# Up scaling, copies and additions of the last batch on ScalarE and GpSimd, with new orders in the last step

## The reference

```python
x = x + tanh(g_xattn) * xattn(layernorm(x), ctx, mask, wq, ...)      # ends in a w8a8 linear: round(o / s) @ qw * (s * sw) + b
h = layernorm(x)
qx, sx = quantize(h)                   # per row: max |h| / 448, values rounded as fp8
g = (qx @ qw_gate.T) * scales;  u = (qx @ qw_up.T) * scales
t = silu(g) * u                        # 1408 columns
qt, st = quantize(t)
x = x + tanh(g_ffn) * (qt @ qw_down.T) * scales
```

## Time and profile before

| | |
|---|---|
| median of three runs | 568.79 us (568.49 to 568.90) |
| the profiled execution's own time | 568.58 us |
| its span in the profile | 566.8 us |
| busy in the span: DVE, ACT, PE, POOL | 487.4, 460.9, 443.5, 226.4 us |
| the last step | from about 466 us to the end |

### The profile page before, as it was taken

The page is one execution under the profiler, slowest core; times in us unless marked ns, Lnnn a source line. Parts: engine busy times, 40 slices in busy tenths (PEclk is TensorE's granted clock), DMA queues, the critical chain, the costliest instruction groups (busy, mean ns, idle before and its releaser), DMA issues.

```text
span 566.8 us, 9844 instructions
## 1 busy us (share of the span) xinstructions
PE 443.5 (78%) x3000; PEld 271.9 (48%) x3030; DVE 487.4 (86%) x1254; ACT 460.9 (81%) x1129; POOL 226.4 (40%) x204
## 2 busy tenths in 40 slices
PE   0397495988898889888988987899889975962945
PEld 0274374555545654565456544564556442531312
DVE  5999789988799889988988798879987987789994
ACT  5679799998989798889898988899889985973451
POOL 4432262004552455245524651546155512442620
PEclk9999897999999999999999999999999999896868
DMA  7942352112213221322133203220421011000111
GB/s 254 386 145 77 105 149 56 39 57 39 56 23 87 74 57 22 87 76 57 26 85 74 57 19 90 76 56 16 94 74 20 19 34 57 19 1 0 26 27 75
DMA packets 62085, 39.52 MB, mean 70 GB/s; under 512 B 47568, under 2 KB 53712, under 8 KB 62032
## 3 DMA queue, kind: packets, MB, share of 16 engines
q1 hardware_dynamic: 58432, 31.67, 20.7%
q0 software_dynamic: 2176, 7.22, 4.2%
q10 hardware_dynamic: 1424, 0.01, 0.1%
HBM read 23.87 MB, written 4.19 MB: 50 GB/s over the span
## 4 chain that ended last, share of the span: by engine, by line
DVE 36%; ACT 15%; POOL 14%; issue 11%; PE 8%; DMA 6%; SPq 1%; DVEq 0%; ACTq 0%; POOLq 0%
POOL up L473 5%; POOL up L463 4%; ACT prob L660 3%; DVE q L1209 3%; POOL x L442 3%; DVE ts L1487 3%; ACT q_last L660 2%; DVE q_last L1310 2%; DVE rows L1426 2%; DVE prob L1310 2%; DVE t_sb L1204 2%; DVE stats L1416 2%; DMA t_sb<-in_L_ffn_w_up_dram,index 2%; ACT rows L576 2%; DVE x2s L1431 2%
## 5 line engine op out<-in xcount | busy, mean ns | idle before, releaser
L463 POOL TENSOR_TENSOR up<-up,wgu_scale 128x512 f32<-128x512 f32 (+1 forms) x42 | 52.1, 1241 | 81.4 <-ACT up L640 81.4
L669 ACT ACTIVATE probT<-bank_h 128x512 f32<-128x512 f32 x128 | 68.5, 588 | 1.1 <-PE bank_h L892 0.9
L660 ACT ACTIVATE prob<-prob,neg_max 128x256 f32<-128x256 f32 x128 | 63.3, 497 | 5.5 <-DVE neg_max L1310 5.5
L660 ACT ACTIVATE q_last<-q_last,neg_max 128x256 f32<-128x256 f32 x128 | 63.4, 500 | 0.5 <-DVE neg_max L1310 0.3
L473 POOL TENSOR_TENSOR up<-gate,up 128x512 f32<-128x512 f32 (+1 forms) x42 | 59.5, 1423 | 3.7 <-DVE gate L1365 1.5
L478 POOL TENSOR_TENSOR x<-x,y 128x512 f32<-128x512 f32 x14 | 19.9, 1424 | 101.8 <-DVE y L1500 101.8
L1310 DVE CUSTOM_DVE_ANT_0 prob<-bank_h,mask_sb 128x256 f32<-128x256 f32 x128 | 47.4, 420 | 13.0 <-PE bank_h L833 13.0
L892 PE MATMUL bank_h<-ident,prob 128*128 128x128 f32 x256 | 39.4, 288 | 14.9 <-ACT prob L660 14.8
L1310 DVE CUSTOM_DVE_ANT_0 q_last<-bank_h,mask_sb 128x256 f32<-128x256 f32 x128 | 47.4, 417 | 0.0
L919 PE MATMUL bank_o<-probT,v_sb 128*32 128x256 f32 x512 | 36.0, 400 | 14.4 <-DVE v_sb L1238 8.0
L833 PE MATMUL bank_h<-kf,qf 32*128 32x256 f32 x512 | 36.7, 400 | 11.7 <-ACT probT L669 11.3
(11 more groups left out here) (235 smaller groups left out, 1199.0 us busy)
## 6 DMA issues: line engine op xcount, KB each, us to landing
x_in<-in_x_dram SPq DMA_DIRECT2D x8, 512.0 KB, 3.6
c_in<-in_ctx_dram SPq DMA_DIRECT2D x8, 512.0 KB, 3.8
out_dram<-x SPq DMA_DIRECT2D x7, 512.0 KB, 3.0
mask_sb<-in_mask_BxSxS_ff_dram SPq DMA_DIRECT2D x8, 256.0 KB, 3.1
t_sb<-in_L_ffn_w_down_dram SPq DMA_DIRECT2D x2, 704.0 KB, 5.8
t_sb<-in_L_ffn_w_down_dram POOLq DMA_DIRECT2D x2, 704.0 KB, 6.8
kf<-in_L_xattn_wq_dram SPq DMA_DIRECT2D x1, 1024.0 KB, 10.9
wkT<-in_L_xattn_wk_dram SPq DMA_DIRECT2D x1, 1024.0 KB, 13.7
```

What stands on the lines that cost most here:

```text
L463: pool.tensor_tensor(up[:, c % 2, 0:w], up[:, c % 2, 0:w], wu_scale[:, off:off + w], ALU.mult).then_inc(f["u_scaled"], 1)
L660: ins = act.activation(prob_of[slot4][:, t, :], prob_of[slot4][:, t, :], ACT.Exp, bias=neg_max[:, slot4, t:t + 1], scale=-1.0, accum_out=r ...
L669: act.activation(probT[:, (slot + 3) % 4, :, :].rearrange("p a b -> p (a b)"), HEAD_BANK[(slot + 3) % 4][:, :], ACT.Copy).then_inc(s["turn ...
```

## The change

- `e`'s up scaling leaves `gate_scale` on DVE; `e` now has `up_copy` on ACT and `up_scale` on POOL, as `k`.
- `oqT_low`, `x2T_copy` and the first `tT_low` of `e` move from DVE to ACT; the second `tT_low` stays on DVE.
- The two additions of `x2_add` and the first of the two final additions (`out_add(13)`) of `e` move from DVE to POOL. The second final addition stays on DVE.
- The last batch is stored in two transfers, one per tile, each when its addition is done.
- The orders of all five engines in the last step are written anew. Semaphores are renamed after what they count (low, high).

The diff, cut: for ACT and PE only the new orders are shown, the old ones stand in the kernel above.

```diff
@@ -364,12 +364,13 @@
...
             def tail_order(k):
-                k.o_turn(0); k.o_turn(1); k.out_store(0); k.x2_turn(0); k.x2_turn(1); k.t_turn(2); k.t_turn(0); k.t_turn(1); k.t_turn(3)
-                k.t_turn(4); k.t_turn(5)
+                k.o_turn(0); k.out_store(0); k.o_turn(1); k.x2_turn(0); k.x2_turn(1); k.t_turn(0); k.t_turn(1)
+                k.t_turn(2); k.t_turn(5); k.t_turn(3); k.t_turn(4)
@@ -379,9 +380,11 @@
...
             sp.dma_start(out[bass.ds(NB - 2, 1)].rearrange("o (t p) c -> p (o t) c", p=P), x2[:, :, :]).then_inc(s["stored"], 16)
-            sp.wait_ge(s_last["out_ready"], 1 + 2)
-            sp.dma_start(out[bass.ds(NB - 1, 1)].rearrange("o (t p) c -> p (o t) c", p=P), x_in[:, :, :]).then_inc(s["stored"], 16)
-            sp.wait_ge(s["stored"], 16 * NB)
+            for t in range(NT):
+                sp.wait_ge(s_last["out_ready"], 1 + t + 1)
+                sp.dma_start(out[bass.ds(NB - 1, 1)].rearrange("o (t p) c -> p (o t) c", p=P)[:, t:t + 1, :],
+                             x_in[:, t:t + 1, :]).then_inc(s["stored"], 16)
+            sp.wait_ge(s["stored"], 16 * (NB + 1))
@@ -437,6 +440,8 @@
...
                 def x2_add(slot):
                     need(pool, s["stored"], 16 * B2)
+                    if not OLD:
+                        pool.wait_ge(s["x_centred"], NB)
                     for t in range(NT):
                         pool.wait_ge(f["y_scaled"], 2 * B2 + t + 1)
@@ -465,10 +470,7 @@
                 def gate_up(slot):
                     c = slot - 6
                     w = CHUNKS[c % NCH][1]
-                    if OLD:
-                        pool.wait_ge(f["u_scaled"], 6 * B2 + c + 1)
-                    else:
-                        pool.wait_ge(f["u_ready"], 1 + 6 * B2 + c + 1)
+                    pool.wait_ge(f["u_scaled"], 6 * B2 + c + 1)
                     pool.wait_ge(f["g_ready"], 1 + 6 * B2 + c + 1)
                     pool.tensor_tensor(up[:, c % 2, 0:w], gate[:, c % 2, 0:w], up[:, c % 2, 0:w], ALU.mult).then_inc(f["gu_ready"], 1)
@@ -493,9 +495,10 @@
             def tail_order(k, e):
                 k.x2_add(1); k.x2_var(2); k.up_scale(6); k.gate_up(6); k.up_scale(7); k.gate_up(7); k.up_scale(8)
-                k.gate_up(8); k.up_scale(9); k.gate_up(9); k.up_scale(10); k.gate_up(10); k.up_scale(11); k.gate_up(11)
-                e.x2_var(2); e.gate_up(6); e.gate_up(7); e.gate_up(8); e.gate_up(9); e.gate_up(10); e.gate_up(11)
-                k.out_add(13); k.out_add(15)
+                k.gate_up(8); k.up_scale(9); k.gate_up(9); k.up_scale(10); k.up_scale(11); e.x2_add(1); k.gate_up(10)
+                k.gate_up(11); e.x2_var(2); e.up_scale(6); e.gate_up(6); e.up_scale(7); e.gate_up(7); e.up_scale(8)
+                e.gate_up(8); e.up_scale(9); e.gate_up(9); e.up_scale(10); e.gate_up(10); e.up_scale(11); e.gate_up(11)
+                k.out_add(13); k.out_add(15); e.out_add(13)
@@ -608,7 +611,24 @@
...
-                    act.activation(turned[:, 2 * N:4 * N], U_BANK[:, :], ACT.Identity, bias=-ROUND).then_inc(f["oq_out_act"], 1)
+                    act.activation(turned[:, 2 * N:4 * N], U_BANK[:, :], ACT.Identity, bias=-ROUND).then_inc(f["oq_out_high"], 1)
+
+                def oqT_low(slot):
+                    act.wait_ge(f["oqT_ps"], d - 1)
+                    act.wait_ge(s["q_ps"], 2 * NB)
+                    act.wait_ge(f["d_ps"], 1 + 2 * B2)
+                    act.activation(turned[:, 0:2 * N], G_BANK[:, :], ACT.Identity, bias=-ROUND).then_inc(f["oq_out_low"], 1)
+
+                def x2T_copy(slot):
+                    act.wait_ge(f["x2T_ps"], d - 1)
+                    act.wait_ge(s["v_ps"], 2 * NB)
+                    act.wait_ge(f["u_ps"], 1 + 6 * B2)
+                    act.activation(x2T[:, :, :].rearrange("p c n -> p (c n)"), half(U_BANK), ACT.Copy).then_inc(f["x2T_ready"], 1)
+
+                def tT_low(slot):
+                    act.wait_ge(f["tT_ps"], 1 + 2 * B2 + 1)
+                    act.wait_ge(s["q_ps"], 2 * NB)
+                    act.activation(turned[:, 0:8 * P], half(G_BANK), ACT.Copy).then_inc(f["tT_out_low"], 1)
 
@@ -764,17 +784,19 @@
 
             def tail_order(k, e):
...
+                k.o_int(0); k.head_probT(0); k.head_exp(0); k.head_exp(1); k.head_exp(2); k.head_exp(3); k.head_probT(1)
+                k.head_probT(2); k.head_probT(3); k.head_probT(4); k.head_exp(4); k.group_oT(1); k.x2_mag_0(3)
+                k.head_exp(5); k.group_oT(5); k.head_exp(6); k.head_exp(7); k.head_probT(5); k.head_probT(6)
+                k.head_probT(7); k.head_probT(8); k.up_copy(6); k.x2_mag_1(3); k.gate_tanh(6); k.head_exp(8)
+                k.up_copy(7); k.head_exp(9); k.head_exp(10); k.up_copy(8); k.gate_tanh(7); k.head_exp(11)
+                k.head_probT(9); k.head_probT(10); k.head_probT(11); k.gate_tanh(8); k.group_oT(9); k.up_copy(9)
+                k.head_probT(12); k.gate_tanh(9); k.group_oT(13); k.t_mag_0(10); k.t_mag_1(10); k.up_copy(10)
+                k.o_round(15); e.oqT_high(0); e.oqT_low(0); k.up_copy(11); k.t_mag_2(11); k.gate_tanh(10); e.x2_mag_0(3)
+                e.x2_mag_1(3); k.gate_tanh(11); e.x2T_copy(5); k.t_mag_0(12); e.up_copy(6); k.t_mag_1(12)
+                e.gate_tanh(6); e.up_copy(7); e.up_copy(8); e.gate_tanh(7); k.t_mag_2(13); e.gate_tanh(8); e.up_copy(9)
+                e.up_copy(10); e.gate_tanh(9); e.t_mag_0(10); e.t_mag_1(10); e.up_copy(11); e.gate_tanh(10)
+                e.gate_tanh(11); e.t_mag_2(11); e.t_mag_0(12); e.t_mag_1(12); e.tT_low(12); e.t_mag_2(13); e.tT_high(12)
+                e.tT_high(14)
@@ -1112,17 +1134,17 @@
             def tail_order(k, e):
...
+                k.head_turn(0); k.head_score(0); k.group_pv(1); k.y_project(0); k.head_turn(1); k.head_turn(2)
+                k.head_turn(3); k.head_turn(4); k.head_score(4); k.group_pv(5); k.head_turn(5); k.head_turn(6)
+                k.head_turn(7); k.head_turn(8); k.up_project(5); k.gate_project(5); k.head_score(8); k.up_project(6)
+                k.gate_project(6); k.group_pv(9); k.head_turn(9); k.up_project(7); k.head_turn(10); k.head_turn(11)
+                k.up_project(8); k.gate_project(7); k.gate_project(8); k.head_turn(12); k.group_pv(13); k.o_turn(14)
+                k.gate_project(9); k.up_project(9); k.up_project(10); k.gate_project(10); e.oqT_turn(0); e.y_project(0)
+                e.x2T_turn(5); e.up_project(5); e.gate_project(5); e.up_project(6); e.gate_project(6); e.up_project(7)
+                e.gate_project(7); e.up_project(8); e.gate_project(8); k.down_project_low(12); e.gate_project(9)
+                e.up_project(9); e.gate_project(10); e.up_project(10); k.down_project_high(12); k.down_project_low(14)
+                k.down_project_high(14); e.tT_turn(11); e.down_project_low(12); e.down_project_high(12); e.tT_turn(13)
...
-                def oqT_low(slot):
...
-                    dve.tensor_scalar(turned[:, 0:2 * N], G_BANK[:, :], ROUND, None, ALU.subtract).then_inc(f["oq_out_dve"], 1)
...
-                def x2T_copy(slot):
...
-                    dve.tensor_copy(x2T[:, :, :].rearrange("p c n -> p (c n)"), half(U_BANK)).then_inc(f["x2T_ready"], 1)
...
                 def tT_low(slot):
-                    t = (slot - 12) // 2
-                    dve.wait_ge(f["tT_ps"], 1 + 2 * B2 + t + 1)
-                    if t == 0:
-                        dve.wait_ge(s["q_ps"], at_most(2 * (b + 1), 2 * NB))
-                    else:
-                        dve.wait_ge(f["d_ps"], 1 + 2 * B2 + 1)
-                    dve.tensor_copy(turned[:, 0:8 * P], half(G_BANK)).then_inc(f["tT_out_dve"], 1)
+                    dve.wait_ge(f["tT_ps"], 1 + 2 * B2 + 2)
+                    dve.wait_ge(f["d_ps"], 1 + 2 * B2 + 1)
+                    dve.tensor_copy(turned[:, 0:8 * P], half(G_BANK)).then_inc(f["tT_out_low"], 1)
 
                 def v_evac(slot):
                     v_out(slot - 11)
...
-                    if not OLD:
-                        dve.wait_ge(f["u_ps"], 1 + 6 * B2 + c + 1)
-                        dve.scalar_tensor_tensor(up[:, c % 2, 0:w], U_BANK[:, 0:w], x2s[:, 5, t:t + 1], wu_scale[:, off:off + w],
-                                                 ALU.mult, ALU.mult).then_inc(f["u_ready"], 1)
...
-                    if not OLD:
-                        dve.wait_ge(s["x_plus_ready"], NB)
-                        dve.wait_ge(s["x_centred"], NB)
-                        for t in range(NT):
-                            dve.wait_ge(f["y_scaled"], 2 * B2 + t + 1)
-                            dve.tensor_tensor(x2[:, t, :], rows[:, t, :], x_plus[:, par, t, :], ALU.add).then_inc(f["x2_ready"], 1)
...
-                    if not OLD:
+                    if not OLD and t == 1:
                         dve.wait_ge(f["y2_ready"], 1 + 2 * B2 + t + 1)
                         dve.tensor_tensor(x2[:, t, :], x2[:, t, :], y2[:, :], ALU.add).then_inc(f["out_ready"], 1)
...
             def tail_order(k, e):
```

(14 more changed lines are left out.)

77 lines of the change are left out of this document (17 added, 60 removed).

## The result

The changed kernel takes 572.13 us (median of 17 runs, 569.0 to 575.08), the kernel before 568.35 beside it (17 runs): ratio 1.0068 [1.0053, 1.0084], slower by about 3.9 us. I had forecast 570.3, slower, in a range of 567.0 to 572.2. 572.13 is just inside it, but the kernel before came out 0.4 us lower this time than the 568.79 that I had forecast from. Measured against that kernel, the change costs 3.9 us and not the forecast's 1.5; carried over to 568.79 it is 572.7, outside. The profiled execution took 570.75 us (span 568.9), only 2.2 more than that of before.

The account below looks back on a forecast made before the run. DVE, busy 487.4 of 566.8 us, was taken to bound the kernel beside the last batch's serial chain. Terms +1.5, +1.6 and -0.5 gave +2.6 us, less 1.1 for port meetings +1.5: 570.3 us, range 567.0 to 572.2.

Parts of the forecast that it names:

- Step 1: Attention part to the end of o_scales: the new orders bring it 0.4 us sooner, bounds +0.5 and -1.2.
- Step 2: To the last batch's statistics: oqT_low on ACT +0.5, y_scale -0.2, additions on POOL +0.7; statistics at 512.4.
- Step 3: Port shared by DVE and POOL: the centring e.x2_centre meets POOL's k.gate_up(11), +0.6 us, bounds 0 and +1.0.
- Step 4: x2T_copy on ACT takes 1.02 us for 0.69, +0.35; the last batch's first gate product comes 1.5 us later.
- Step 5: Last batch's first gate product to batch 6's second down product: 25.2 us, +1.6 with port waits, bounds -1.2 and +2.5.
- S: Mark on TensorE, first gate product of the last batch: 522.14 before, forecast 1.5 us later at 523.6.
- The discount in the sum: Only two thirds of the two port terms (0.6 and 2.8 us) taken, 1.1 us less, as not every meeting is paid.
- the port's share: DVE and POOL port waits before batch 6's second down product: 2.8 us, from S + 25.2 to S + 22.4 if free.
- Step 6: The rest: last matmuls at 1.2 GHz again and tT_low on ACT 0; smaller last store -0.5 us, bounds 0 and -0.8.
- The sum fully paid: Whole change with every meeting at the port paid: +1.5 + 1.6 - 0.5 = +2.6 us.
- Rival C: Everything late: all port meetings paid, no gain before o_scales, up to 1 us for TensorE's clock; 571.8 to 572.8; chance 0.16.
- Rival A: Relief wins: DVE and POOL rarely meet, 8.3 us off DVE shows; -1.2 to -1.9 us, likeliest 567.2; chance 0.28.

Follow-up runs that it names:

- Experiment 3: Changed kernel with the SyncE, ScalarE, TensorE and VectorE orders of the kernel before up to the last o_scales; 569.53 us, ratio 1.0020.
- 1 and 2: Changed kernel with the early store behind both transposes again (570.99 us; reverse in the kernel before, 569.53), and with the y product behind two probability transposes (570.26 us).
- a_mag_early: Changed kernel with x2_mag_1 put back ahead of head_probT(5) on ACT, and x2_sum_1 and x2_sub_1 ahead of mask 8 on DVE; ratio 1.0083.
- 7: Kernel before with only the last batch's two x2 additions moved to GpSimd, ahead of its last gate-up product of batch 6; 571.16 us, ratio 1.0048.
- a_store_late: Changed kernel with SyncE's store of the batch before put back behind both transposes of the attention output; 570.99 us, ratio 1.0038.
- a_gate7_mag_store: Changed kernel with head_turn(11), gate_scale(7), the second tile's magnitudes and sums, and the store behind both transposes put back; ratio 1.0088.
- a_y_behind_turns: Changed kernel with TensorE's y_project(0) moved back behind head_turn(1) and head_turn(2); 570.26 us, ratio 1.0044.
- b_store_between: Kernel before with SyncE's store placed between the two transposes of the attention output; 569.53 us, ratio 1.0001.
- a_turns_in_order: Changed kernel with SP's last three transposes of the rounded rows issued 3, 4, 5 instead of 5, 3, 4; 572.04 us, ratio 1.0038.

## Why the prediction failed

Its steps in its own order, sizes against what the table shows (one profile each):

- **Step 1, attention part: -0.4 forecast (bounds -1.2 and +0.5), +1.91 measured.** This is the step that failed. I had followed the lists as though an item ahead of its place only gains, and read the last probability product 0.4 sooner; it came 1.9 later. Experiment 3 shows that the order does it. Score 8 comes 0.31 later and the interval behind it is 1.60 longer. The interval is the sure part; the 0.31 is less than what score 8 moves between executions (+24.5 or +25.4 with the lists of before). For score 8, 1 and 2 show the y product standing for a transpose beside the store, with TensorE's clock down behind that wait: without it score 8 is 0.3 sooner than before, where I had read 1 to 2 us. I named such a gap in the bound, but ahead of the second probability product, and gave it 0.5. For the interval I had only x2_sum_1 and x2_sub_1 ahead of mask 10, and let the sooner scores pay for it; but with those two taken out of there it stays at 11.59 (a_mag_early), so which items make it longer stays open.
- **Step 2, to the statistics: right.** Forecast 512.4, which is 8.2 behind the forecast o_scales; measured 8.18. Its +0.7 for the additions depended on GpSimd being free by then, as 7 shows.
- **Step 3, the centring: +0.6 forecast, +0.25 measured** (1.15 for two at 516.17, where the kernel before has 0.90):

```profile
513.43 0.90 DVE L1426 TENSOR_SCALAR rows<-x_in,mv_last 128x512 f32<-128x512 f32 x2
```

- **Step 4: right.** With the copy on ScalarE (1.02 us) front is +1.54; steps 2 to 4 fully paid gave +1.9 behind o_scales, less the 0.35 of step 3.
- **Step 5, mid: 25.2 forecast, 25.09 measured.** The last rounding of batch 6 ends at S + 19.9 (forecast 20.3) and the down product 5.2 us behind it (forecast 4.9). So the number, with every meeting at the port paid, held. **The discount in the sum did not**: it took 0.9 us off this term, which was right, and 0.2 off step 3's, the only one that was too large. What is not shown is the port's share: the working put it at 2.8 us, down to S + 22.4 if both engines ran freely, but with the scalings cut to 64 columns mid fell only to 24.29. The rule that the Trainium skill's "SBUF — State Buffer" states in "SBUF: two separate sides", an exclusive lock held by whichever starts first, agrees with the trace here: the 1.76 us row at 530.11 ends at 531.87, which is 0.55 behind the end of GpSimd's gate-up product (529.74 to 531.32), as in the earlier trace rows.
- **Step 6: 0 and -0.5 forecast; -0.24 and -0.77 measured.** Of tile 1's -1.68 I had nothing.

The sum fully paid was +2.6. Step 1 adds 2.3, step 3 and the small ones take 1.0, which gives the 3.9. Rival C, everything late, comes nearest (571.8 to 572.8, chance 0.16), but in part by luck: all meetings were paid as it said, but it had the attention part at nothing and not at +1.9, and its last microsecond was to come from TensorE at 1.2 GHz in the middle stretch, where the granted clock was 0.91 against 0.79 in the earlier trace rows. The direction, slower, was right, though my largest miss had the wrong sign. Rival A fell: VectorE's relief shows as 3.0 us less busy on the page (484.4 against the earlier trace rows), while 22.36 of mid's 25.09 us are busy, port waits included. The forecast of what the rows would show (over 1 us beside GpSimd, centring over 1 us, the down product at S + 25, a short last store) held but for S, 2.0 us later than its 1.5.

## What to carry to other kernels

The orders of five engines' lists are one object: moving one or a few items cost up to 4.8 us by the ratios where the whole set cost 2.7, so the bound on a reordered part is what one wrong position costs (1.3 to 4.2 us of one interval here, where it cost anything), not the gains that one sees. Work moved off the busiest engine brought nothing here, where its new engine takes 1.3 us for its 0.75, stands at the same port and hands back within the same chain. A discount on a cost worked out from rows needs a row of its own. And two single profiles give a term's sign sooner than its size: compare each term with other executions of the same code first.

## What the runs showed of the hardware

- A 512 KB store and two transposes on one queue: with the store behind both it landed in 2.9 or 3.0 us in six kernels and in 5.0 and 4.8 in two (a_store_late, a_gate7_mag_store). With the store between, the transposes' median was 3.6 us in ten kernels and 2.8 in two (a_y_behind_turns, b_store_between), against 2.4 with the store behind. The order alone does not decide it.
- TensorE's clock falls to 1.2 GHz behind a wait of some 2.7 us in a stretch that otherwise stays at 2.4 GHz (0.64 mean from 473 to 476 us against 1.00). How long it stays low behind the longer wait that follows differs between executions of the same code: it is at 2.4 GHz from 23 us behind the zero in after, and at 1.2 GHz nearly to 26 in a_turns_in_order, with 1.4 us of att between them.
- Single profiled executions of one code differ by 1.7 us in the last tile's chain (6.5 or 8.2), by 0.8 to 1.4 in att and by 0.8 in mid, so the profiles' own difference (+2.2) was a poor measure of the medians' (+3.9).
